# Transposes of both heads behind the value matmuls, in the first layer's attention

## The chip, the cores and the metric

The kernel runs on one core of a Trainium2 chip. The metric is the device time of one execution in microseconds. Lower is better. The engines are TensorE (PE in the rows, its weight loads PEld), VectorE (DVE), ScalarE (ACT), GpSimd (POOL) and SyncE (SP).

## What is computed

Two transformer layers on x of 2 x 1024 tokens by 128 features, all in f32. Each layer is attention and a feed-forward part, each with layer norms before and behind it. The first layer's attention, which the change is about:

```
q, k, v = proj(wq), proj(wk), proj(wv)          # 16 heads of 64
scores = einsum('bhqd,bhkd->bhqk', q, k) * 64 ** -0.5
scores = where(causal, scores, -inf)
probs = softmax(scores)
out = einsum('bhqk,bhkd->bhqd', probs, v)
return einsum('bse,he->bsh', out, wo)
```

Behind it come a mixture of 8 experts, an attention with 16 heads of 8 and rotary positions, and a ternary-weight feed-forward part.

## The kernel before

The first layer's 16 heads go in 8 turns of two heads (`HPC` is 2). A turn has 16 query tiles of 128 rows, 8 for each batch row b. A tile qt needs the keys of tiles 0 to qt, so its cost grows with qt + 1. The order of tiles in a turn is qt 0, 4, 1, 5, 2, 6, 3, 7 for b = 0 (the first half), then 7, 3, 6, 2, 5, 1, 4, 0 for b = 1: large tiles (qt 4 to 7) and small ones (0 to 3) alternate. A tile's two heads are a pair of items, the even head 2p and the odd head 2p + 1. Softmax sums are taken out at the end of each half.

An item passes through these operations (line numbers of the kernel before):

- scores on TensorE (L1100), a product with the high and one with the low part of the keys, into `pS`, which has two buffers, so that item i waits for the maximum of item i - 2
- maximum on VectorE (L828), which also writes the masked scores to `probs`, which has three buffers (`NPROB`): item i waits for the transposes of item i - 3
- exponential on ScalarE (L605), in place in `probs`, with its sum read out behind it
- transposes on TensorE (L1133), one for each key tile, at most four to a round. A round takes one of three banks `pT` (`TBANKS`) and waits for the copy of the round three before it. Items of large tiles take two rounds, of small ones one.
- copy of each round to `PT` in SBUF, by ScalarE (L585) or VectorE (L862), in turn by the number of the round
- value matmuls for both heads of a pair (L1063), then VectorE's copy of the result (L787)

The projections of the coming batch row or turn are rounds too ("P", L1025 for queries and keys, L1029 for values), twelve in a turn, copied by ScalarE (L553, L561). They stand at odd steps.

All engines run an in-order program that is written out step by step. `Attention.__init__` makes the table of rounds: `at_step[i]` lists the rounds of step i, and each engine's loop over i follows it. In an even step i TensorE issues the scores of items i and i + 1. In an odd step it issues the value matmuls of the pair i - 5, i - 4. In each step it then waits for the exponential of item i - 2 and issues the rounds of the table. ScalarE's step is its exponential of item i and then the copies of the step's rounds. VectorE's step is the output copy, the maximum of item i, and then its copies.

Of the kernel before, what the change touches and what calls it, by code (L numbers as in the profile page):

```python
# [24 lines left out]
T = B * S  # L25
# [3 lines left out]
TPB = BANK // P  # L29
# [3 lines left out]
HPC = P // DH0  # L33
# [49 lines left out]
class Attention:  # L83
# [3 lines left out]
    def __init__(self, heads, turns, copies, project):  # L87
        self.heads = heads
        tiles = list(range(ST)) if heads > 2 else [t + h * (ST // 2) for t in range(ST // 2) for h in range(2)]
        order = [(0, qt) for qt in tiles] + [(1, qt) for qt in reversed(tiles)]  # L90
        self.order = [(c, b, qt) for c in range(turns) for b, qt in order]
        self.items = [(c, b, qt, h) for c, b, qt in self.order for h in range(heads)]
        self.n = len(self.items)
        self.per = self.n // turns
        self.rounds = []
        self.at_step = [[] for _ in range(self.n + 8)]
        self.copied = {"act": 0, "dve": 0}
        self.round_of = {}
        self.done_by = []
        if project:  # L100
            for u in range(6):
                self.project(0, 0, 0, u)
            self.at_step[0] = []
        self.ahead = len(self.rounds)
        for step in range(self.n + 8):
            if 2 <= step < self.n + 2:
                c, b, qt, h = self.items[step - 2]
                for k0 in range(0, qt + 1, TPB):
                    self.add(step, "T", (step - 2, k0, min(TPB, qt + 1 - k0)), [copies[len(self.rounds) % len(copies)]])
                self.round_of[step - 2] = len(self.rounds) - 1  # L110
            if project:
                c, at = divmod(step, self.per)
                for c2, b2, start in ((c, 1, 1), (c + 1, 0, self.per // B + 1)):
                    u, odd = divmod(at - start, 2)
                    if 0 <= u < 6 and not odd and c2 < turns:
                        self.project(step, c2, b2, u)
            self.done_by.append(dict(self.copied))
# [1218 lines left out]
```

How the kernel before makes its waits and increments, by code:

```python
            def halves(c, b):  # L354
                lo, hi = slice(0, DH0), slice(DH0, P)
                if (c, b) == (0, 0):
                    sp.wait_ge(A[0]["cp_dve"], plan.projected(c, b, 0, 1, "dve"))
                else:
                    sp.wait_ge(split_step, 2 * HPC * (plan.split_number(c, b, 0, 1) + 1))
                sp.dma_start(Qs[hi, b, 0, :].bitcast(F32), Ql[lo, b, :].bitcast(F32)).then_inc(ld_half[b], 16)
                sp.dma_start(Qs[lo, b, 1, :].bitcast(F32), Ql[hi, b, :].bitcast(F32)).then_inc(ld_half[b], 16)
                if (c, b) == (0, 0):
                    sp.wait_ge(A[0]["cp_dve"], plan.projected(c, b, 1, 1, "dve"))
                else:
                    sp.wait_ge(split_step, 2 * HPC * (plan.split_number(c, b, 1, 1) + 1))
                for kx in (Kh, Kl):
                    sp.dma_start(kx[hi, b, 0, :].bitcast(F32), kx[lo, b, 0, :].bitcast(F32)).then_inc(ld_half[b], 16)
                    sp.dma_start(kx[lo, b, 1, :].bitcast(F32), kx[hi, b, 1, :].bitcast(F32)).then_inc(ld_half[b], 16)
# [1 line left out]
            def spread(half):  # L371
                sp.wait_ge(turned_copied, half + 1)
                sp.dma_start(factors[half, :, :].rearrange("h (t q) -> (h t) q", q=P), factorsT[:, :]).then_inc(factors_out, 16)
                if half == 0:
                    sp.wait_ge(q_p, 5 * (FC1 + 1))
                else:
                    sp.wait_ge(rescaled, half)
                sp.wait_ge(factors_out, 16 * (half + 1))
                for h in range(HPC):
```

## Time and profile before

| | us |
|---|---|
| median of 3 runs | 1271.85 (1269.1 to 1274.05) |
| profiled execution | 1276.66 |
| its span | 1274.7 |
| TensorE busy | 1114.3 (87%) |
| VectorE busy | 869.6 |
| ScalarE busy | 817.2 |
| GpSimd busy | 348.9 |

The first layer's attention lies at about 45 to 562 us of the span, the experts behind it, and the second layer's attention at about 830 to 1200 us. TensorE's records overlap, since matmuls are pipelined: the distance between starts is its pace, the mean duration is not.

### The profile page before, as it was taken

How to read it: one execution, taken by the hardware profiler on the slowest of the kernel's cores; microseconds unless marked ns; L12 is line 12 of the kernel's file. 1: busy time of each engine (PE TensorE's matmuls, PEld its weight loads, DVE VectorE, ACT ScalarE, POOL GpSimd, SP SyncE). 2: the span in 40 equal slices, each digit the busy share in tenths (PEclk: the TensorE clock that was granted, in tenths of full speed). 3: DMA queues.
4: the chain of work that ended last, by engine and by line, in shares of the span. 5: the costliest groups of instructions: out<-in, count | busy, mean ns of one | idle time of the engine just before them, and what ended most of it. 6: DMA issues, size and time to landing. Idle time of an engine off the chain costs nothing.

```text
span 1274.7 us, 28360 instructions
## 1 busy us (share of the span) xinstructions
PE 1114.3 (87%) x10202; PEld 850.3 (67%) x10202; DVE 869.6 (68%) x2512; ACT 817.2 (64%) x1915; POOL 348.9 (27%) x345
## 2 busy tenths in 40 slices
PE   2799999999999999998999951688888888888886
PEld 1587888787878787888676730456556556556674
DVE  3565656565656665645433476799899999999863
ACT  2566666666666666631434223789889989989832
POOL 1597464646464545313000051000000000000033
PEclk9899999999999999998899976799899999899998
DMA  3222232323232222211000004311302202100001
GB/s 107 70 60 62 69 73 59 83 57 84 57 76 66 69 72 68 67 35 42 5 17 25 5 1 118 56 24 17 39 12 29 38 4 37 27 14 2 2 1 33
DMA packets 29671, 56.74 MB, mean 45 GB/s; under 512 B 4538, under 2 KB 14674, under 8 KB 29410
## 3 DMA queue, kind: packets, MB, share of 16 engines
q1 hardware_dynamic: 28738, 53.43, 18.8%
q8 instruction: 80, 1.31, 0.4%
q10 hardware_dynamic: 800, 1.57, 0.4%
q14 instruction: 53, 0.43, 0.1%
HBM read 25.49 MB, written 4.33 MB: 23 GB/s over the span
## 4 chain that ended last, share of the span: by engine, by line
PE 55%; DVE 19%; issue 11%; ACT 6%; POOL 5%; DMA 3%; SPq 1%; ACTq 0%; POOLq 0%; DVEq 0%
PE pT L1133 12%; PE pO L1063 11%; PE pS L1100 10%; DVE Zb L818 9%; PE pS L1195 4%; PE pT L1025 4%; PE pT L1207 3%; DVE Sm L833 3%; ACT probs L605 3%; PE pS L1156 2%; PE pT L1029 2%; PE pS L1293 1%; PE pS L1273 1%; ACT PT L585 1%; DMA KS<-split 1%
## 5 line engine op out<-in xcount | busy, mean ns | idle before, releaser
L1133 PE MATMUL pT<-cst,probs 128*128 128x128 f32 x2304 | 368.8, 286 | 55.2 <-ACT probs L605 53.2
L1133 PEld LDWEIGHTS pT<-cst,probs 128*128 128x128 f32 x2304 | 255.5, 142 | 151.9 <-ACT probs L605 104.0
L605 ACT ACTIVATE probs<-probs,nmax 128x128 f32<-128x128 f32 (+7 forms) x256 | 198.8, 776 | 131.7 <-DVE nmax L828 130.7
L585 ACT COPY PT<-pT 128x512 f32<-128x512 f32 (+3 forms) x576 | 263.7, 481 | 16.1 <-PE pT L1133 14.7
L828 DVE CUSTOM_DVE_ANT_0 probs<-pS,causal_wide 128x128 f32<-128x128 f32 (+7 forms) x256 | 192.1, 750 | 92.8 <-PE pS L1100 85.2
L1063 PE MATMUL pO<-PT,V 128*64 128x128 f32 (+1 forms) x4608 | 230.6, 277 | 1.9 <-DVE attnT L787 1.1
L605 ACT ACTIVATE probs<-Sm,nmax 128x128 f32<-128x128 f32 (+7 forms) x256 | 199.2, 778 | 29.3 <-DVE nmax L833 22.3
L818 DVE TENSOR_SCALAR Zb<-pS 128x128 bf16<-128x128 f32 (+7 forms) x256 | 192.8, 753 | 24.4 <-PE pS L1106 24.1
L461 POOL TENSOR_TENSOR rstd<-rstd,power 128x4 f32<-128x4 f32 x32 | 32.8, 1025 | 628.0 <-DVE rstd L725 627.4
L1063 PEld LDWEIGHTS pO<-PT,V 128*64 128x64 f32 (+1 forms) x4608 | 179.9, 113 | 33.8 <-issue 19.6
L833 DVE CUSTOM_DVE_ANT_0 Sm<-pS,Zb 128x128 f32<-128x128 f32 (+7 forms) x256 | 193.3, 755 | 4.5
L862 DVE COPY PT<-pT 128x256 f32<-128x256 f32 (+3 forms) x192 | 99.9, 520 | 115.9 <-PE pT L1133 114.5
L1100 PE MATMUL pS<-Kh,Qs 128*128 128x512 f32 (+2 forms) x384 | 159.0, 423 | 7.2 <-DMA Kl<-Kl 7.2
L1100 PE MATMUL pS<-KS,QS 72*128 72x512 bf16 (+3 forms) x384 | 109.0, 338 | 36.0 <-DMA KS<-split 31.9
L1100 PE MATMUL pS<-Kl,Qs 128*128 128x512 f32 (+2 forms) x384 | 128.8, 344 | 0.0
L1100 PEld LDWEIGHTS pS<-Kh,Qs 128*128 128x128 f32 x384 | 73.3, 191 | 27.8 <-issue 21.7
L1100 PEld LDWEIGHTS pS<-Kl,Qs 128*128 128x128 f32 x384 | 73.5, 191 | 20.3 <-issue 14.6
L645 ACT ACTIVATE hT<-pS,b1e 128x512 f32<-128x512 f32 x64 | 43.9, 687 | 57.5 <-PE pS L1195 57.3
L504 POOL TENSOR_TENSOR Kl<-raw,Kh 64x512 fp32r<-64x512 f32 x60 | 76.5, 1276 | 4.8
L504 POOL TENSOR_TENSOR Ql<-raw,Qs 64x512 fp32r<-64x512 f32 x60 | 76.5, 1275 | 4.8
L524 POOL TENSOR_TENSOR attnT<-attnT,wq_t 128x1024 f32<-128x1024 f32 x16 | 37.9, 2370 | 117.6 <-DMA wq_t<-factors 117.0
L976 DVE SCALAR_TENSOR_TENSOR acc<-pT,wcol,acc 128x128 f32<-128x128 f32 x96 | 27.0, 344 | 61.7 <-PE pT L1207 61.7
(185 smaller groups left out, 1376.2 us busy)
## 6 DMA issues: line engine op xcount, KB each, us to landing
Qs<-Ql SPq DMA_DIRECT2D x32, 256.0 KB, 3.7
Kh<-Kh SPq DMA_DIRECT2D x32, 256.0 KB, 3.4
Kl<-Kl SPq DMA_DIRECT2D x32, 256.0 KB, 4.6
wq_t<-factors SPq DMA_DIRECT2D x32, 256.0 KB, 3.9
QS<-split SPq DMA_DIRECT2D x72, 64.0 KB
KS<-split SPq DMA_DIRECT2D x72, 64.0 KB
w0s<-in_w SPq DMA_DIRECT2D x8, 192.0 KB, 4.1
split<-parts SPq DMA_DIRECT2D x2, 768.0 KB, 3.5
```

The lines of the kernel that those rows point to most:

```text
L504: i = pool.tensor_tensor(low[h], source[rows[h], :], high[h].bitcast(F32), ALU.subtract)
L585: nc.scalar.copy(PT[:, g % 2, h, k0 * P:(k0 + nk) * P], pT[r % TBANKS][:, 0:nk * P])\
L605: nc.scalar.activation(probs[:, i % NPROB, 0:n], src[:, 0:n], ACT.Exp, bias=nmax[:, i % 4:i % 4 + 1], scale=-1.0, accum_out=total).then_in ...
L818: nc.vector.tensor_scalar(Zb[:, i % NMASK, 0:n], pS[i % 2][:, 0:n], 0.0, MASKED, ALU.is_equal, ALU.mult).then_inc(a["z"], 1)
L828: nc.vector.tensor_tensor_reduce(probs[:, i % NPROB, 0:n], pS[i % 2][:, shift(k, qt):shift(k, qt) + n], causal_wide[:, S - n:S], -1.0, 3e3 ...
L833: nc.vector.tensor_tensor_reduce(Sm[:, i % NMASK, 0:n], pS[i % 2][:, 0:n], Zb[:, i % NMASK, 0:n], -(DH1 ** -0.5), 3e38, ALU.add, ALU.min, ...
L862: nc.vector.tensor_copy(PT[:, gg % 2, hh, k0 * P:(k0 + nk) * P], pT[r % TBANKS][:, 0:nk * P])\
L1025: return nc.tensor.matmul(p, w0s[:, what, :], xnT[:, b * S + j * BANK:b * S + (j + 1) * BANK], start=True, stop=True)
L1063: m = nc.tensor.matmul(pO[rows, 0:P], v, PT[:, g % 2, h, kt * P:(kt + 1) * P], start=(kt == 0), stop=(kt == qt), skip_group_check=True)
L1100: m = nc.tensor.matmul(pS[i % 2][:, (off + c0) * P:(off + c1) * P], lhs, keys[:, b, h, c0 * P:c1 * P], start=(n == 0), stop=(n == len(rhs) ...
L1133: m = nc.tensor.transpose(pT[r % TBANKS][:, kt * P:(kt + 1) * P], probs[:, item % NPROB, (k0 + kt) * P:(k0 + kt + 1) * P], ident)
L1195: nc.tensor.matmul(bank[u % 4], w1s[:, buf, f * P:(f + 1) * P], xnT[:, j * BANK:(j + 1) * BANK], start=True, stop=True).then_inc(up_done, 1)
```

## The change

The table of rounds is made differently for a layer whose heads go in twos. The transposes of item i - 2 stood in step i, so the even head's in an even step behind the scores and the odd head's in the next step behind the value matmuls. Now both stand in the odd step. In the even step TensorE issues only scores. Line numbers below the change grow by 3. The second layer's attention has `heads` = 4 and takes the first branch, its old order.

```diff
         for step in range(self.n + 8):
-            if 2 <= step < self.n + 2:
-                c, b, qt, h = self.items[step - 2]
+            ready = [step - 2] if heads > HPC else [step - 3, step - 2] if step % HPC == 1 else []
+            for item in ready:
+                if not 0 <= item < self.n:
+                    continue
+                c, b, qt, h = self.items[item]
                 for k0 in range(0, qt + 1, TPB):
-                    self.add(step, "T", (step - 2, k0, min(TPB, qt + 1 - k0)), [copies[len(self.rounds) % len(copies)]])
-                self.round_of[step - 2] = len(self.rounds) - 1
+                    self.add(step, "T", (item, k0, min(TPB, qt + 1 - k0)), [copies[len(self.rounds) % len(copies)]])
+                self.round_of[item] = len(self.rounds) - 1
```

On TensorE, in the first turn, before, behind the scores of qt 3: the transposes of qt 6's even head (7, to banks pT2 and pT0), the values of qt 2, and the transposes of qt 6's odd head (pT1 and pT2). In brackets the semaphores that a row waits for, `a0_cp_act` and `a0_cp_dve` for copies, `a0_p` for exponentials.

```order
97 L1133 MATMUL pT2<-cst,probs_57 128x128 [waits a0_cp_dve,a0_p]
98 L1133 MATMUL pT2<-cst,probs_57 128x128 x3
99 L1133 MATMUL pT0<-cst,probs_57 128x128 [waits a0_cp_act]
100 L1133 MATMUL pT0<-cst,probs_57 128x128 x2
101 L1063 MATMUL pO<-PT0_55,V0_54 64x128 [waits a0_cp_dve,a0_cp_act,a0_n]
102 L1063 MATMUL pO<-PT0_55,V0_54 64x128 x5
103 L1133 MATMUL pT1<-cst,probs_57 128x128 [waits a0_cp_act,a0_p]
104 L1133 MATMUL pT1<-cst,probs_57 128x128 x3
105 L1133 MATMUL pT2<-cst,probs_57 128x128 [waits a0_cp_act]
106 L1133 MATMUL pT2<-cst,probs_57 128x128 x2
```

The same place with the change:

```order
97 L1066 MATMUL pO<-PT0_55,V0_54 64x128 [waits a0_cp_act,a0_cp_dve,a0_n,a0_p]
98 L1066 MATMUL pO<-PT0_55,V0_54 64x128 x5
99 L1136 MATMUL pT2<-cst,probs_57 128x128 [waits a0_cp_dve,a0_p]
100 L1136 MATMUL pT2<-cst,probs_57 128x128 x3
101 L1136 MATMUL pT0<-cst,probs_57 128x128 [waits a0_cp_act]
102 L1136 MATMUL pT0<-cst,probs_57 128x128 x2
103 L1136 MATMUL pT1<-cst,probs_57 128x128 [waits a0_cp_act]
104 L1136 MATMUL pT1<-cst,probs_57 128x128 x3
105 L1136 MATMUL pT2<-cst,probs_57 128x128 [waits a0_cp_act]
106 L1136 MATMUL pT2<-cst,probs_57 128x128 x2
```

The values moved ahead of all four rounds. The first and the fourth round both take pT2, and between them nothing but two rounds of transposes is left. The wait for exponentials stands at the values (for the even head) and at the first transposes (for the odd one).

On ScalarE, before, behind qt 6's two exponentials (128x896) to those of qt 7 (128x1024), with the exponentials of qt 3 (128x512) and the first round's copy of each head of qt 6:

```order
34 L605 ACTIVATE probs_57,den0<-probs_57,nmax 128x896 [waits a0_mx] x2
35 L585 COPY PT0_55<-pT0 128x384 [waits a0_o,a0_t]
36 L561 COPY V0_54<-pT1 128x512 [waits a0_t]
37 L605 ACTIVATE probs_57,den0<-probs_57,nmax 128x512 [waits a0_mx]
38 L585 COPY PT0_55<-pT2 128x512 [waits a0_o,a0_t]
39 L605 ACTIVATE probs_57,den0<-probs_57,nmax 128x512 [waits a0_mx]
40 L585 COPY PT0_55<-pT1 128x512 [waits a0_o,a0_t]
41 L605 ACTIVATE probs_57,den0<-probs_57,nmax 128x1024 [waits a0_mx]
```

With the change:

```order
32 L608 ACTIVATE probs_57,den0<-probs_57,nmax 128x896 [waits a0_mx] x2
33 L588 COPY PT0_55<-pT0 128x384 [waits a0_o,a0_t]
34 L564 COPY V0_54<-pT1 128x512 [waits a0_t]
35 L608 ACTIVATE probs_57,den0<-probs_57,nmax 128x512 [waits a0_mx] x2
36 L588 COPY PT0_55<-pT2 128x512 [waits a0_o,a0_t]
37 L588 COPY PT0_55<-pT1 128x512 [waits a0_o,a0_t]
38 L608 ACTIVATE probs_57,den0<-probs_57,nmax 128x1024 [waits a0_mx] x2
```

The copy from pT2 stood between the two exponentials of qt 3, and now stands behind both.

## Rows read from the trace of the kernel before

**Rows 1.** Busy time by engine, granted clock, DMA share, GB/s, one stretch
```profile
200.00:330.00 130.00, 129.75 (x1158) 105.40 (x1157) 79.07 (x217) 87.17 (x200) 69.73 (x68) 1.00 0.28 69
```
**Rows 2.** Waits of TensorE and its weight loads, 72 to 560 us
```profile
PE pS L1100 <- DMA Kl<-Kl: 0.5, 1, 0.5
PE pO L1063 <- DVE attnT L787: 0.5, 1, 0.5
PE pT L1133 <- ACT PT L585: 0.4, 1, 0.4
...
PEld pT L1133 <- ACT probs L605: 7.9, 46, 0.2
```
**Rows 3.** Timeline of TensorE and its loads: start, us, what, idle before
```profile
333.76 0.39 PE L1100 MATMUL pS<-Kh,Qs 128*128 128x512 f32 x1
333.99 0.40 PE L1100 MATMUL pS<-Kl,Qs 128*128 128x512 f32 x1
...
334.69 1.04 PE L1133 MATMUL pT<-cst,probs 128*128 128x128 f32 x8
335.66 1.09 PE L1063 MATMUL pO<-PT,V 128*64 128x128 f32 x16
337.61 1.02 PE L1025 MATMUL pT<-xnT,w0s 128*128 128x512 f32 x2
...
335.65 0.85 PEld L1063 LDWEIGHTS pO<-PT,V 128*64 128x64 f32 x16 [0.17 <-issue]
336.68 0.86 PEld L1133 LDWEIGHTS pT<-cst,probs 128*128 128x128 f32 x8 [0.17 <-ACT probs L605]
```
**Rows 4.** Line 796: duration ns min/median/max, first and last start us
```profile
L796 DVE RECIPROCAL rden<-den x16: 241/243/247, 76.0 to 558.6; 128x16 f32<-128x16 f32 x16
```
**Rows 5.** VectorE: groups by shape, 72 to 560 us, then timeline pieces
```profile
L828 DVE CUSTOM_DVE_ANT_0 probs<-pS,causal_wide 128x1024 f32<-128x1024 f32 x30 | 36.2, 1207 | 3.2 <-PE pT L1133 1.6 <-PE pS L1100 1.2
...
L828 DVE CUSTOM_DVE_ANT_0 probs<-pS,causal_wide 128x512 f32<-128x512 f32 x30 | 20.6, 686 | 14.0 <-PE pS L1100 13.8 <-issue 0.2
...
L828 DVE CUSTOM_DVE_ANT_0 probs<-pS,causal_wide 128x128 f32<-128x128 f32 x30 | 8.1, 270 | 0.5 <-PE pS L1100 0.5
...
326.14 0.08 DVE L828 DVE_READ_ACCUMULATOR2_ANT nmax<- 128x1 f32 x1
...
335.76 0.69 DVE L862 COPY PT<-pT 128x512 f32<-128x512 f32 x1 [0.57 <-PE pT L1133]
```
**Rows 6.** ScalarE: groups by shape, 72 to 560 us, then timeline pieces
```profile
L585 ACT COPY PT<-pT 128x512 f32<-128x512 f32 x109 | 62.4, 572 | 8.6 <-PE pT L1133 8.5
...
L605 ACT ACTIVATE probs<-probs,nmax 128x1024 f32<-128x1024 f32 x31 | 35.6, 1150 | 30.0 <-DVE nmax L828 30.0
...
L605 ACT ACTIVATE probs<-probs,nmax 128x512 f32<-128x512 f32 x30 | 21.7, 724 | 9.3 <-DVE nmax L828 9.3
...
L605 ACT ACTIVATE probs<-probs,nmax 128x128 f32<-128x128 f32 x30 | 12.0, 401 | 7.8 <-DVE nmax L828 7.8
...
L585 ACT COPY PT<-pT 128x128 f32<-128x128 f32 x15 | 3.7, 246 | 0.0
...
326.26 0.72 ACT L605 ACTIVATE probs<-probs,nmax 128x512 f32<-128x512 f32 x1 [0.44 <-DVE nmax L828]
326.89 0.19 ACT L605 ACTIVATION_READ_ACCUMULATOR probs<-probs,nmax 128x1 f32 x1
326.99 0.56 ACT L585 COPY PT<-pT 128x512 f32<-128x512 f32 x1
```
**Rows 7.** Timeline of ScalarE and TensorE's loads at a copy waited for
```profile
310.67 0.58 ACT L585 COPY PT<-pT 128x512 f32<-128x512 f32 x1
...
311.30 0.14 PEld L1133 LDWEIGHTS pT<-cst,probs 128*128 128x128 f32 x1 [0.17 <-ACT PT L585]
```
**Rows 8.** Second layer: busy time by engine and clock, two stretches
```profile
860.00:880.00 20.00, 17.76 (x260) 13.81 (x249) 19.83 (x36) 19.05 (x42) 0.00 (x0) 1.00 0.21 27
...
900.00:920.00 20.00, 17.03 (x129) 10.32 (x130) 16.30 (x72) 16.48 (x62) 0.00 (x0) 0.74 0.46 57
```

## Prediction

> **What bounds the kernel now.** I read the busy times by stretch first. In the first layer's attention (about 45 to 562 us) TensorE is busy for 129.75 of 130 us at a granted clock of 1.00, with VectorE at 79 and ScalarE at 87 us [rows 1]. That alone could be an illusion, since matmul ends are modelled, so next the waits: in 488 us TensorE's matmuls wait 0.5 us for a DMA, 0.5 us for VectorE and 0.4 us for ScalarE, and its weight loads 7.9 us for exponentials, never over 0.2 us at a time [rows 2]. So no chain through other engines is late: every result is there when TensorE's in-order program comes to it. Whatever the change takes from that slack is free until it is used up, and then costs in full, because the engines that would be waited for stand in series and TensorE has nothing else to issue.
>
> **TensorE's own pace.** In [rows 3] eight transposes (L1133) take 334.69 to 335.66, of which 8 x 0.107 us are streaming and about 0.11 the change to the value matmuls (L1063); those take 335.66 to 336.68 for 16 records (0.053 each) and 0.17 for the change back, as the weight loads' idle 0.17 shows. Value matmuls leave two records per instruction, so a tile with n key tiles costs 4n x 0.053 us. Scores (L1100) go at 0.23 per 512 columns (333.76 to 333.99), a 512-column projection (L1025) takes 0.86. By such intervals a turn (16 tiles, two heads each) sums to 62.0 us: scores 17.4, transposes 15.4, values 15.4, projections 8.6, about 0.28 of switching and 0.05 of first-score delay in each of 16 pairs. Measured are 15 halves between the reciprocals at 76.0 and 558.6 us, 64.3 us a turn [rows 4]. I keep the 2.3 us of difference as bubbles I cannot place.
>
> **What the change does.** Nothing is added or removed: same matmuls, exponentials, copies, DMAs; the second layer (`heads > HPC`) keeps its order. The switches between 128- and 64-column matmuls stay two a pair (scores to values, values to transposes), so the 0.28 us stays. SP's and GpSimd's queues keep their order; their transfers and splits follow the loop's pace, whatever that is. What moves is the even head's transposes, from before the value matmuls to behind them, and on ScalarE and VectorE the even head's copies, from before the odd head's exponential and maximum of the next pair to behind them. Call the pair whose transposes run P and the next pair N. Three waits change:
>
> (a) The odd maximum of N overwrites the `probs` buffer of P's even head (three buffers), so it waits for P's even transposes. These were issued right after the scores; now they stand behind the value matmuls.
>
> (b) `pT` has three banks, and a large tile (qt 4 to 7) needs two rounds a head, four a pair. The fourth round takes the bank of the first, so it waits for the first round's copy. Before, that copy was made between N's two exponentials, while the value matmuls ran. Now it stands behind N's odd exponential on ScalarE (or N's odd maximum on VectorE), which by (a) can't begin before P's even transposes are done. So within one block of transposes TensorE waits for: end of even transposes, odd maximum, odd exponential, copy. Nothing is left to cover it but one round of four transposes.
>
> (c) Even transposes now also wait for their own pair's odd exponential.
>
> **Cost of (b).** From the end of streaming of the even transposes: 0.21 us until the next engine can begin (335.55 to 335.76, [rows 3, 5]); the maximum m; 0.04 to the exponential (326.22 to 326.26) [rows 5, 6]; from its start to the copy's start x, which is the row's mean duration (326.26 to 326.99 for 0.724); the four-tile copy, 0.572; 0.05 until TensorE goes on (311.25 to 311.30) [rows 7]. Against it stand 4 x 0.107 of transposes. The stall is 0.44 + m + x. m is 0.270, 0.686, 1.207 for 1, 4 and 8 key tiles, x 0.401, 0.724, 1.150 [rows 5, 6]; between those I interpolate straight.
> A worked one, qt 6 in the first half, N being qt 3: 0.44 + 0.686 + 0.724 = 1.85 us.
> Banks and engines alternate by round number; counting rounds (6 ahead, then 60 a turn), the first round's copy is ScalarE's for the first half's large tiles and for qt 4 of the second. The others: qt 4 (N is qt 1) 0.44+0.41+0.51 = 1.36; qt 5 (N 2) 0.44+0.55+0.62 = 1.61; qt 7 (N is the other batch's qt 7) 0.44+1.21+1.15 = 2.80; second half's qt 4 (N 0) 0.44+0.27+0.40 = 1.11.
> For the second half's qt 7, 6, 5 VectorE copies the first round, and the projection round behind them waits for ScalarE's copy c of the second, which decides: 0.30 + m + x + c less the odd transposes already streamed. qt 7 (N 3): 0.30+0.69+0.72+0.57-0.86 = 1.43; qt 6 (N 2): 0.30+0.55+0.62+0.46-0.75 = 1.18; qt 5 (N 1): 0.30+0.41+0.51+0.36-0.64 = 0.94. The shorter copies c are on the line between 0.246 (one tile) and 0.572.
> Sum of a turn: 1.36+1.61+1.85+2.80+1.43+1.18+0.94+1.11 = 12.3 us.
> Small tiles need two rounds and never meet this wait.
>
> **Cost of (a) and (c).** After a small tile's transposes the next large pair's odd maximum and exponential follow, in place of which TensorE streams odd transposes, a projection, two scores and the small tile's values. For second-half qt 4 behind qt 1 without a projection: transposes 0.21, 0.21, maximum 0.82 give 1.24 plus about 0.05, while TensorE reaches the odd score (pS needs that maximum) at 0.43+0.28 = 0.71, so 0.6 late. For the others the same sum gives 0 to 0.2. Together 0.9 us a turn.
>
> **Sum.** 13.2 us x 8 turns = 105 us on the profiled execution's 1276.7, so 1382; the runs' median is 4.8 us under that execution, so **1377 us**. Bounds: if the 2.3 us a turn of unplaced bubbles lie where the stalls fall, 10.9 x 8 = 87 and 1359. If operations that here overlap by 0.09 (the copy at 326.99 starts before the read of the sum ends at 327.08) come one behind another, and ScalarE, which must first do the previous small copy, a projection copy (0.6) and N's even exponential, is itself late by some 0.4 in the five cases where it copies the first round, a turn costs 13.2 + 8 x 3 x 0.09 + 5 x 0.4 = 17.4, or 1411. The clock I leave at 1.00: the second layer's stretch at 17.76 of 20 us busy has it [rows 8], and the loop here would be busy for 64 of 78.
>
> **Rivals.**
> *Hidden after all.* The copies come earlier than I think, and only (a) and (c) cost: 0.9 x 8 = 7, so 1279. For it speaks that ScalarE and VectorE are idle a third of the time; against it that (b) is a chain in series, which idle engines don't shorten. 5%.
> *Faster.* One of the block changes disappears: transposes to values cost 0.11 us, 128 pairs x 0.11 = 14, so 1258. It needs scores to values to be free, and (b) to cost under 0.11 us a pair on average, where I have 0.8; above that it is slower. That the cause is the array's shape and not the instruction kind fits the 0.17 us in both directions. 3%. (The Trainium skill, "TensorEngine Tiling (Array Packing)", Key Properties, says that a change of tiling mode drains the engine; by that rule the new order keeps both drains and this rival is worth nothing.)
> *Clock.* The new stalls of 1 to 3 us cut TensorE's work into bursts and the granted clock falls. In a stretch of the second layer with heavy DMA traffic it was 0.74 [rows 8]; at that, 64.3 us of work in a turn become 87, +22.6 x 8 = 181 on top of 1377, so 1558. Against it: the second layer's other stretches keep 1.00 at 17 to 18 busy of 20 us [rows 8]. 5%. (The Trainium skill, "TensorE: Matmul & The Clock Gate", under the psum-queue depth-cycling failure, says that short idle spells between groups of matmuls, from cycling through banks, were seen to make the clock swing between its levels. By it the time would go towards this rival. The trace shows no such loop in the first layer.)
> *Slower by far less*: two thirds of the chain hidden by work I put in the wrong place, 1300 to 1340. 6%.
> The forecast's mechanism has the remaining 81%.
>
> **Numbers.** 1377 is the likeliest mechanism's time; 1345 to 1425 takes in both bounds with some room, and leaves the rivals, 19%, outside. A difference under 0.5% (6 us) can't be told from none. Faster 3% (that rival), same 3% (the better part of the hidden one), slower 94%.
>
> **What would show it.** Right: between 45 and 660 us TensorE waits for ScalarE's PT copies (L588) some 35 to 40 times by 1 to 3 us and for VectorE's or ScalarE's behind the rest; VectorE's maximum (L831) waits for transposes; reciprocals lie 38.7 us apart instead of 32.2; clock 1.00; everything behind the attention has its old lengths. Wrong: transposes without a wait between third and fourth round (then (b) is no chain), a granted clock under 0.9 there (the clock), or waits at the exponential larger than at the copies (then (c) is mis-sized).

## The result, and the profile after

The kernel with the change takes 1484.55 us (median of 4 runs, 1480.91 to 1487.43), against 1272.95 before: ratio 1.1663, interval 1.1621 to 1.1705. It is slower by 212 us. I had forecast slower by 105, 1377 in a range of 1345 to 1425. The direction is right, the size is not.

All of it lies in the first attention. VectorE's reciprocals come once a half, so the stretch between the first and the last of the 16 holds 7.5 turns. The first row is that line's in the kernel after, then come the busy times and the granted clock of that stretch:

```profile
L799 DVE RECIPROCAL rden<-den x16: 242/248/249, 84.5 to 772.9; 128x16 f32<-128x16 f32 x16
...
84.50:772.90 688.40, 533.11 (x4341) 413.52 (x4341) 288.53 (x811) 324.21 (x745) 248.84 (x242) 0.95 0.19 46
```

The stretch of before (76.0 to 558.6, [rows 4]) has this row:

```profile
76.00:558.60 482.60, 480.51 (x4326) 391.47 (x4322) 294.72 (x810) 323.13 (x745) 255.57 (x246) 1.00 0.27 66
```

It grew by 205.8 us: 153.2 of TensorE's idle time (155.3 against 2.1) and 52.6 of its busy time. ScalarE's and VectorE's busy times are the old ones, so nothing got longer there. The granted clock fell from 1.00 to 0.95, which I had left at 1.00. The waits of TensorE's matmuls in that stretch (us in total, times, longest), which answer to [rows 2]:

```profile
PE pT L1136 <- ACT PT L588: 64.5, 40, 2.7
PE pO L1066 <- ACT raw L556: 27.8, 21, 1.7
PE pO L1066 <- ACT V L564: 20.7, 14, 1.6
PE pT L1136 <- DVE PT L865: 20.0, 21, 1.1
PE pO L1066 <- ACT PT L588: 15.6, 18, 1.2
PE pS L1103 <- DVE nmax L831: 5.8, 10, 0.6
```

The reciprocals lie 45.9 us apart, where the forecast had 38.7. Three groups are to be seen. Transposes (pT) wait for copies 61 times, 84.5 us: the fourth round's wait, (b) of the prediction. Scores (pS) wait for the maximum, 5.8 us: the small wait I had for second-half tiles. And value matmuls (pO) wait 53 times for ScalarE's copies, 64.1 us, at small tiles (qt 0 to 3). That group is nowhere in the prediction.

**The fourth round, in the trace.** TensorE, ScalarE and VectorE of the kernel after, in the first half of a turn, from qt 6's transposes on (start, us, what, idle before):

```profile
349.91 1.42 PE L1136 MATMUL pT<-cst,probs 128*128 128x128 f32 x11
351.05 0.27 PE L1136 MATMUL pT<-cst,probs 128*128 128x128 f32 x1
353.11 0.55 PE L1136 MATMUL pT<-cst,probs 128*128 128x128 f32 x3 [1.78 <-ACT PT L588]
...
351.77 0.72 ACT L608 ACTIVATE probs<-probs,nmax 128x512 f32<-128x512 f32 x1 [2.21 <-DVE nmax L831]
352.40 0.18 ACT L608 ACTIVATION_READ_ACCUMULATOR probs<-probs,nmax 128x1 f32 x1
352.49 1.05 ACT L588 COPY PT<-pT 128x512 f32<-128x512 f32 x2
...
351.04 0.69 DVE L831 CUSTOM_DVE_ANT_0 probs<-pS,causal_wide 128x512 f32<-128x512 f32 x1 [2.94 <-PE pT L1136]
```

Eleven transposes run, three rounds; the second row is the last of them by itself. The odd maximum of qt 3 begins at 351.04, 2.94 us after VectorE last had work, the exponential at 351.77, the copy at 352.49, and TensorE goes on at 353.11. The last of the eleven starts at 351.05, and such records start 0.11 us apart, so its streaming ends at 351.16 and the hole is 1.95 us where 1.85 was predicted. The row shows 1.78, since the modelled end of the last matmul (351.05 + 0.27) lies 0.17 behind its streaming. I call these 0.17 us the hidden tail of a wait.

**The values' wait, in the trace.** The same three engines one pair earlier, qt 2's transposes and the values of qt 2 behind the scores of qt 3:

```profile
345.03 0.88 PE L1136 MATMUL pT<-cst,probs 128*128 128x128 f32 x6
345.74 1.06 PE L1032 MATMUL pT<-w0s,xnT 128*128 128x128 f32 x8
346.55 0.47 PE L1103 MATMUL pS<-Kh,Qs 128*128 128x512 f32 x1
...
349.10 0.88 PE L1066 MATMUL pO<-PT,V 128*64 128x128 f32 x12 [1.37 <-ACT V L564]
...
345.72 1.09 DVE L831 CUSTOM_DVE_ANT_0 probs<-pS,causal_wide 128x896 f32<-128x896 f32 x1 [1.77 <-PE pT L1136]
...
346.86 1.04 ACT L608 ACTIVATE probs<-probs,nmax 128x896 f32<-128x896 f32 x1 [1.74 <-DVE nmax L831]
...
347.90 0.46 ACT L588 COPY PT<-pT 128x384 f32<-128x384 f32 x1
348.26 0.58 ACT L564 COPY V<-pT 128x512 f32<-128x512 f32 x1
```

Qt 2's even transposes are the first three of the six from 345.03, and the odd maximum of qt 6, which waits for them, starts at 345.72. Its exponential starts at 346.86. Behind it ScalarE makes qt 2's copy and the projection's copy, until 348.84, and only then may the values start, at 349.10. The scores were issued from 346.55 on and had nothing left by 347.7. It is the same chain, transposes, odd maximum, odd exponential, copies, with another customer at its end.

**The clock, in the trace.** Three stretches of the kernel after around one of its eight longest stalls, and the work behind that stall:

```profile
360.00:364.00 4.00, 2.96 (x30) 2.17 (x28) 1.84 (x4) 2.14 (x5) 0.00 (x0) 1.00 0.00 0
364.00:368.00 4.00, 1.55 (x5) 1.25 (x6) 1.65 (x4) 2.20 (x4) 0.00 (x0) 0.77 0.00 0
368.00:372.00 4.00, 4.00 (x36) 2.76 (x36) 1.19 (x4) 1.41 (x3) 1.88 (x3) 0.81 0.02 4
...
366.45 1.12 PE L1136 MATMUL pT<-cst,probs 128*128 128x128 f32 x4 [2.74 <-ACT PT L588]
367.36 1.92 PE L1028 MATMUL pT<-xnT,w0s 128*128 128x512 f32 x2
368.29 1.40 PE L1103 MATMUL pS<-Kh,Qs 128*128 128x512 f32 x1
```

After 2.74 us without a matmul four transposes take 0.91 us to the next row instead of 0.43: the lower of the two levels, 1.2 GHz. The projection behind them is just as slow. Seven of the eight stalls of 2.74 us have such slow work behind them. Behind the one that ends at 456.83 the clock stayed at 1.00.

The clock also falls where no long stall is, in the second half of a turn, at qt 1 and the tiles behind it:

```profile
122.77 0.44 PE L1136 MATMUL pT<-cst,probs 128*128 128x128 f32 x2 [0.80 <-DVE PT L865]
128.25 0.38 PE L1103 MATMUL pS<-Kh,Qs 128*128 128x256 f32 x1 [0.58 <-DVE nmax L831]
129.67 0.66 PE L1066 MATMUL pO<-PT,V 128*64 128x128 f32 x8 [0.91 <-ACT PT L588]
...
128.00:132.00 4.00, 2.83 (x19) 2.23 (x19) 1.44 (x9) 1.80 (x6) 0.00 (x0) 0.83 0.01 4
132.00:136.00 4.00, 3.35 (x24) 2.99 (x25) 0.89 (x5) 1.72 (x6) 0.00 (x0) 0.50 0.00 0
136.00:140.00 4.00, 4.00 (x25) 2.62 (x22) 1.53 (x6) 1.58 (x5) 1.06 (x2) 0.82 0.00 0
```

From about 130.5 to 137.5 us the clock is at the lower level, behind three stalls of under 1 us each. This comes back at the same place in six of the first seven turns, and once elsewhere in the last turn (748 to 752 us, behind stalls of 0.51 and 1.22 us). The fifth turn has the same stalls there (0.58 and 0.91 us, at 405.15 and 406.56) and keeps 1.00. Read in half microseconds, each one's busy time times what its clock lacks of 1.00, the slow work sums to an estimated 31 us in the stretch: 11 behind seven of the long stalls and 20 at the other seven places.

### The profile page after: what moved, and what is told of

The parts are those of the page before. It is cut to its first block, busy times and chain, and to the rows that moved or that the text cites. A ratio compares the mean times of both kernels' runs of the same rounds, so it can differ in the third digit from the quotient of the medians.

```text
span 1485.5 us, 28357 instructions
## 1 busy us (share of the span) xinstructions
PE 1163.8 (78%) x10202; PEld 868.0 (58%) x10202; DVE 862.6 (58%) x2512; ACT 816.8 (55%) x1915; POOL 347.8 (23%) x345
## 4 chain that ended last, share of the span: by engine, by line
PE 47%; issue 20%; DVE 18%; ACT 10%; DMA 2%; POOL 1%; SPq 1%; DVEq 0%; ACTq 0%; POOLq 0%
PE pO L1066 12%; PE pT L1136 10%; DVE Zb L821 8%; PE pS L1103 7%; ACT PT L588 4%; ACT probs L608 4%; PE pT L1028 3%; PE pS L1198 3%; PE pT L1210 3%; DVE Sm L836 3%; PE pS L1159 2%; PE pS L1296 1%; DMA KS<-split 1%; PE pS L1276 1%; PE pO L1210 1%
## 5 line engine op out<-in xcount | busy, mean ns | idle before, releaser
L1066 PE MATMUL pO<-PT,V 128*64 128x128 f32 (+1 forms) x4608 | 237.4, 281 | 69.0 <-ACT raw L556 29.2
L588 ACT COPY PT<-pT 128x512 f32<-128x512 f32 (+3 forms) x576 | 259.2, 481 | 8.7 <-PE pT L1136 6.3
L1066 PEld LDWEIGHTS pO<-PT,V 128*64 128x64 f32 (+1 forms) x4608 | 187.2, 116 | 111.3 <-issue 58.8
L1103 PE MATMUL pS<-Kh,Qs 128*128 128x512 f32 (+2 forms) x384 | 168.3, 445 | 13.1 <-DMA Kl<-Kl 6.7
L1103 PE MATMUL pS<-Kl,Qs 128*128 128x512 f32 (+2 forms) x384 | 131.8, 350 | 0.0
L504 POOL CAST Qs<-raw 64x512 fp32r<-64x512 f32 x60 | 36.5, 608 | 269.6 <-ACT raw L556 267.2
L1028 PE MATMUL pT<-xnT,w0s 128*128 128x512 f32 x128 | 77.0, 691 | 1.1 <-ACT xnT L546 0.7
```

The source lines that it names most:

```text
L588: nc.scalar.copy(PT[:, g % 2, h, k0 * P:(k0 + nk) * P], pT[r % TBANKS][:, 0:nk * P])\
L1028: return nc.tensor.matmul(p, w0s[:, what, :], xnT[:, b * S + j * BANK:b * S + (j + 1) * BANK], start=True, stop=True)
L1066: m = nc.tensor.matmul(pO[rows, 0:P], v, PT[:, g % 2, h, kt * P:(kt + 1) * P], start=(kt == 0), stop=(kt == qt), skip_group_check=True)
L1103: m = nc.tensor.matmul(pS[i % 2][:, (off + c0) * P:(off + c1) * P], lhs, keys[:, b, h, c0 * P:c1 * P], start=(n == 0), stop=(n == len(rhs) ...
```

## The experiments

Eleven kernels ran. Each ratio is to the kernel before on the same chip. The edits are shown against the kernel with the change, and `...` stands for lines left out.

### Is the odd maximum's wait the root?

Four `probs` buffers in the first layer, the changed order. To make room, the weights of the first two experts share space with `Kl` and are loaded behind the attention.

```diff
-REGION = 160
+REGION = 164
...
+        self.nprob = 4 if heads == HPC else NPROB
...
-                        if i >= NPROB:
-                            dve.wait_ge(a["t"], plan.round_of[i - NPROB] + 1)
+                        if i >= plan.nprob:
+                            dve.wait_ge(a["t"], plan.round_of[i - plan.nprob] + 1)
```

> The order of the change, but with four probs buffers in the first layer, so that the odd maximum no longer waits for the even transposes of the pair before. (The weights of the first two experts are loaded behind the attention to make room.) Theory A, that this one wait is the root and the waits for copies at the fourth round and at the value matmuls only descend from it: the time comes back to that of before, 1262 to 1290 us, and the waits for copies in the first attention fall from 150 us to under 20. Theory B, that the copies' place behind both exponentials in ScalarE's order is enough by itself to make TensorE wait: 1340 us or more, with most of the waits for copies left.

Measured: 1307.09 us, ratio 1.0289 (1.0246 to 1.0332). Of 212 us 177 are gone with one more buffer and not one instruction moved on any engine's compute path. TensorE's waits in the stretch between the reciprocals:

```profile
PE pT L1137 <- ACT PT L589: 8.4, 14, 0.9
PE pO L1067 <- ACT raw L557: 7.0, 21, 0.6
PE pO L1067 <- DVE attnT L791: 3.2, 10, 0.5
PE pO L1067 <- ACT V L565: 2.8, 7, 0.4
```

The waits for copies are 18 us, as theory A had it, and B falls, though its queue order is unchanged here. But the time isn't back at 1272 and lies above A's range (1262 to 1290). A has a remainder of 35 us to explain.

The control has the same buffers and late load in the order of before.

> The order of before with four probs buffers and the late load of the experts' weights: the control for the kernel with four buffers in the new order, which took 1307. All theories: 1268 to 1276, since TensorE waits for nothing there. If this too is near 1305, the 35 us lie in the buffers or the late load, not in the order.

Measured: 1274.65 us, ratio 1.0012 (0.9993 to 1.0032). So the 35 us belong to the order.

### One part of the change alone

The rule that decides which even heads are moved, here for the large tiles; the small tiles' kernel has `< TPB`.

```diff
-            ready = [step - 2] if heads > HPC else [step - 3, step - 2] if step % HPC == 1 else []
+            late = lambda item: 0 <= item < self.n and self.items[item][2] >= TPB
+            if heads > HPC:
+                ready = [step - 2]
+            elif step % HPC == 1:
+                ready = [step - 3, step - 2] if late(step - 3) else [step - 2]
+            else:
+                ready = [] if late(step - 2) else [step - 2]
```

> Only the large tiles' (qt 4 to 7) even transposes are moved behind the value matmuls, the small tiles keep the order of before. If the fourth round's wait and the value matmuls' wait are separate costs (theory A): the bank waits stay (84 us), the value waits go, and with 10 to 25 us for the lower clock behind the long stalls the time is 1365 to 1385. If the two feed each other, either part alone costs clearly less than its share, so under 1350.

Measured: 1407.61 us, ratio 1.1057 (1.1015 to 1.1099), 22 us above the range. The waits of its stretch:

```profile
PE pT L1142 <- ACT PT L594: 67.4, 40, 2.7
PE pT L1142 <- DVE PT L871: 20.0, 21, 1.2
PE pO L1072 <- ACT raw L562: 8.0, 21, 0.7
```

The transposes' waits are those of the whole change (87.4 against 84.5), so the fourth round's wait belongs to the large tiles alone. What I had set too low was all that comes with it: busy time of 510.27 in the stretch against 480.51, and 14 us at the values. Its clock (0.98) falls only behind the eight longest stalls.

> Only the small tiles' (qt 0 to 3) even transposes are moved. Theory A: no fourth round is in them, so no bank wait; the value matmuls of the small tile wait for copies behind the large tile's odd exponential, about 65 us, and the odd scores 6 us: 1335 to 1355. My prediction on record had only 7 us for this part: 1275 to 1285.

Measured: 1326.14 us, ratio 1.0429 (1.0391 to 1.0468). It lies between the two numbers, nearer to theory A's. But the waits are not where I had put them:

```profile
PE pT L1142 <- ACT PT L594: 22.5, 46, 1.0
PE pS L1109 <- DVE nmax L837: 5.8, 10, 0.6
PE pO L1072 <- DVE attnT L796: 2.1, 7, 0.3
```

Not one is at the values for a copy. Here the large tile's even transposes still stand between the scores and the small tile's values. They wait for the late copies in the values' place, and cover part of the time. So the parts are not independent: alone they cost 135 and 54 us, 189 together, and the whole 212. Most of the 23 us between goes with the clock. By the same half microseconds the slow work is 12.5 us with the large tiles alone, none with the small tiles alone (the clock is 1.00 all through), and 31 with both.

### ScalarE's order

```diff
-                    if k == 0:
+                    if k == 0 and i % HPC == 0:
                         exponential(i)
                         rounds_out(i)
```

> The order of the change, but ScalarE makes the copies of an odd step before its exponential, not behind it; VectorE keeps its order. Theory A: the 65 us of waits for ScalarE's copies at the fourth round and most of the waits at the value matmuls go, those for VectorE's copies (20 us) stay, and the odd exponential, now behind the copies, makes the next transposes wait by some 0.5 to 1 us for large pairs: 1330 to 1400. Theory B, that ScalarE's order alone is the cause: 1275 to 1300.

Measured: 1346.99 us, ratio 1.0597 (1.0555 to 1.064). ScalarE's queue order is worth 138 us while the maximum is late, so it is a condition of the chain. (The clock of the stretch is 1.00 here, so the 138 us hold the 31 of slow work.) It isn't all of it: 75 us remain, and the rows name VectorE, whose copies still stand behind its odd maximum.

```profile
PE pT L1136 <- DVE PT L865: 20.0, 21, 1.2
PE pT L1028 <- DVE PT L865: 6.2, 7, 0.9
PE pS L1103 <- DVE nmax L831: 5.8, 10, 0.6
```

### The values' wait

The values of a pair one pair later in the first layer, so that their copies have more time.

```diff
+        self.queued = 6 if heads == HPC else QUEUED
...
-                    if plan.ends_group(i - QUEUED):
-                        values(k, plan.group(i - QUEUED), i)
+                    if plan.ends_group(i - plan.queued):
+                        values(k, plan.group(i - plan.queued), i)
```

> The order of the change, but in the first layer the value matmuls of a pair (and the copy of their result) come one pair later than now, so that the copies they wait for have one more pair's time. Theory A, that the values' wait for copies behind the odd exponential is the term missing from the prediction (64 us of waits by the trace, about 78 with the pipeline's tail): these waits vanish, the 84 us at the fourth round stay, and the time is 1390 to 1420. Theory C, that TensorE waits for the chain through maximum and exponential wherever the values stand: the wait only moves to the next transposes or scores, and the time is over 1450.

Measured: 1408.78 us, ratio 1.1069 (1.1042 to 1.1096), 75.8 us less than the change, as theory A had it. Its rows have no wait for a copy at the values, and at the transposes the old ones:

```profile
PE pT L1137 <- ACT PT L589: 66.7, 40, 2.7
PE pT L1137 <- DVE PT L866: 19.8, 21, 1.1
PE pS L1104 <- DVE nmax L832: 6.1, 10, 0.9
```

Theory C, that the wait only moves on, falls. The 75.8 us aren't the values' wait alone, though: the stretch's clock rose from 0.95 to 0.98. All eight long stalls still have slow work behind them, the other places have none, and the slow work is 13 us where it was 31. On the other side TensorE has 9 us more idle time elsewhere (100.0 us in all, where 155.3 less the 64.1 would leave 91.2).

The projection's copy by itself: `done_by` is recorded ahead of the projections of a step, so that the values wait for the transposes' copies alone.

```diff
+            self.done_by.append(dict(self.copied))
             if project:
...
-            self.done_by.append(dict(self.copied))
```

> The order of the change, but the value matmuls wait only for the copies up to the transposes of their step, not for the projection's copy behind them. Of the 53 waits at the values 35 ended with a projection's copy, which takes about 0.5 us behind the transposes' copy on ScalarE: 17 us less, 1460 to 1475. If those waits are really for the exponential ahead of them all, at most this; if nothing changes (over 1480), they are for VectorE's copy, which ends at about the same time.

Measured: 1448.93 us, ratio 1.1379 (1.1346 to 1.1411), 36 us less than the change and twice what I expected. The waits did what was expected: 46.7 us at the values for copies, 17.4 less than 64.1. The rest is in the busy time, 517.35 against 533.11, at a clock of 0.98 against 0.95. With the shorter waits the clock stayed up more. (The profile is of the slowest of its four runs, 1457.81 us.)

The control for the later values, in the order of before:

> The order of before with the value matmuls one pair later, the control for the two kernels that have it: TensorE waits for nothing in the first attention either way, so 1268 to 1278.

Measured: 1314.22 us, ratio 1.0344 (1.0314 to 1.0373). The expectation missed it by 36 us. Waits in 80 to 560 us:

```profile
DVE PT L863 <- PE pO L1064: 137.9, 75, 2.8
...
ACT PT L586 <- PE pO L1064: 63.9, 54, 1.9
```

`PT` has two buffers, so a copy waits for the values of the pair two before. With the values one pair later, in the old order the even head's transposes come ahead of just those values: their copies can't be made, and the banks stay full. The transposes wait 23.6 us for copies in the stretch (0.4 before). In the changed order the transposes stand behind the values, and the setback doesn't arise. Distance helps there and hurts here.

### The clock

Eight dummy transposes in front of each large pair's third round. They add work to TensorE, and their result is overwritten.

```diff
-                        for r in plan.at_step[i]:
+                        for at, r in enumerate(plan.at_step[i]):
...
+                                if k == 0 and at == 2 and plan.items[item][2] >= TPB:
+                                    for _ in range(8):
+                                        nc.tensor.transpose(pT[r % TBANKS][:, 0:P], cst[:, C_UPPER:C_UPPER + P], ident)
```

> The order of the change plus eight dummy transposes (0.86 us of TensorE's time, result overwritten) ahead of each large pair's third round, that is inside the stall before the fourth round (0.9 to 2.8 us). If the granted clock of 0.95 costs nothing: 1480 to 1490, since the dummies fill waiting time. Theory A, that idle spells of 2 to 3 us lower the clock and the slow work behind them costs some 20 us: the clock rises towards 1.00 and the time falls to 1462 to 1478. If the dummies are not hidden: 1484 + up to 64 x 0.86 = 1539.

Measured: 1466.25 us, ratio 1.1536 (1.1502 to 1.157), 18.3 us less than the change, with more work. The stretch, and the first of its waits:

```profile
82.70:748.60 665.90, 559.64 (x4829) 447.56 (x4829) 289.56 (x811) 323.74 (x745) 248.97 (x242) 1.00 0.19 48
...
PE pT L1139 <- ACT PT L588: 32.4, 39, 1.9
```

The clock is back at 1.00 with the 27.6 and 20.7 us of waits at the values still there, and one slow piece is left (126.7 to 130.7 us). The dummies take the place of idle time at every fourth round: its waits fall from 84.5 to 34.0 us, the longest from 2.7 to 1.9 us and those for VectorE's copies from 20.0 to 1.6. So it is idle time before the fourth round without which the clock hardly falls. This run doesn't tell the long stalls from the short ones, and the trace of the change has slow work behind both.

### What is left with four buffers

> The order of the change with four probs buffers and with the value matmuls one pair later. With four buffers alone it took 1307, with 13 us of waits at the value matmuls, 8 us for ScalarE's copies at the transposes and 13 us more busy time than before. Theory A: the values' waits go with the greater distance, the 8 us stay: 1285 to 1295, not under the kernel before. If a burst of both heads' transposes costs nothing in itself and the rest of the 35 us was all at the values: 1268 to 1278.

Measured: 1291.17 us, ratio 1.0144 (1.0117 to 1.0171). Later values take 16 of the 35 us.

> As the kernel with four buffers and later values, and ScalarE makes an odd step's copies before its exponential. The remaining waits at the fourth round were for copies that stood behind an exponential (8 us of waits, some 15 with the pipeline's tail): 1272 to 1284. If it is over 1290, the rest of the loss lies in the burst itself: a round's copy (0.57 us) against the three rounds of transposes that cover it.

Measured: 1292.77 us, ratio 1.0176 (1.015 to 1.0203). ScalarE's order is worth nothing any more: the 4.8 us that transposes waited for its copies are gone, and 4.6 us for its now later exponentials have come. A queue order that cost 138 us behind a late maximum costs none behind an early one. Its stretch is 504.0 us long, against 482.6 before. The wait for a copy or an exponential that is left in it:

```profile
PE pT L1138 <- ACT probs L610: 4.6, 7, 0.7
```

That some 20 us remain, mostly in gaps too short to be listed as waits, I read as the burst's own price: a first round's copy needs 0.21 + 0.57 + 0.05 = 0.83 us, and the rounds that cover it are back to back. The waits of the weight loads, which stand ahead of the matmuls, point the same way: 12.0 us for copies of transposes, 37 times and never over 0.4, where the kernel before has 1.8, and 17.0 us for exponentials, where it has 7.9. That is 19 us more, but no run takes the burst apart by itself, so the reading is argued, not shown. No version here beats the kernel before.

## Why the prediction was wrong

The forecast was 105 us slower, the result is 212.

**The chain (b) and its price were right.** The prediction summed it to 12.3 us a turn, 98 for eight. The stretch begins behind qt 4, 5 and 6 of the first turn, so 93 for its 61 waits. Measured are 84.5 us of waits and 61 hidden tails of 0.17, 95 us, and by an estimate from three of them (those that end at 98.31, 111.40 and 122.77 us) another 2 to 3 before the projection rounds behind, about 98. One by one: 1.95 measured for 1.85 at qt 6, and 2.90 for 2.80 at qt 7:

```profile
363.44 0.27 PE L1136 MATMUL pT<-cst,probs 128*128 128x128 f32 x1
366.45 1.12 PE L1136 MATMUL pT<-cst,probs 128*128 128x128 f32 x4 [2.74 <-ACT PT L588]
```

The 0.10 too little in both is one step: from the end of the even transposes to the odd maximum it takes 0.31 us (350.73 to 351.04), and the prediction had taken 0.21 from a copy. Its root was right too, (a): one more buffer removed 177 of 212 us.

**The step that failed is "Cost of (a) and (c)".** It said that after a small tile "TensorE streams odd transposes, a projection, two scores and the small tile's values", and priced only the odd score's wait for the maximum (0.6 us forecast; the row at 128.25 has 0.58, 0.75 with its tail). It passed over the values themselves. They wait for the copies of the pair and of the projection round behind it, and these copies stand behind the odd exponential by the same delay as in (b). With 0.9 us a turn it had 7 us for this whole part. The values' waits alone are 64.1 us and 53 tails of 0.17 (the scores ahead of them have the same tail, 347.33 + 0.40 against 347.33 + 0.23), 73 us. The forecast's own sentence on what moves, "the even head's copies, from before the odd head's exponential", names the delay, and I priced it for one of its two customers.

**"The clock I leave at 1.00"** failed as well. The reason given was that the second layer holds 1.00 at 17.76 busy of 20 us, but [rows 8] has a stretch at 17.03 of 20 beside it with 0.74, so the busy share alone didn't tell the two apart. The slow work is an estimated 31 us, and the filler got 18.3 back. Part of the difference is that waits behind slow work are shorter: the fourth round of the second half's qt 4 waits 0.65 us at 132.79, where the clock is low, and 1.06 at 409.41, where it isn't. The rival on the clock had named the cause, but its 181 us took 0.74 for the whole stage. (The Trainium skill, "TensorE: Matmul & The Clock Gate", in the part on psum-queue depth-cycling, tells of a clock that swings when TensorE idles between groups. This trace agrees in kind, with 0.77 and 0.81 behind a stall of 2.74 us, and 0.50 behind stalls of 0.80, 0.58 and 0.91 us.) What exactly makes the clock fall stays open: the same stalls had slow work behind them in most turns and not in the fifth.

**Sum.** In the stretch 98 (fourth round), 73 (values), 31 (clock) and 7.5 (scores, with their tails) make some 209, where it grew by 205.8 us. The first part agrees with the forecast within some 5%; the second and the third are in no term of it. An experiment that takes one part away moves the others too, so its gain isn't that part: the 75.8 us of the later values hold some 18 of the clock.

**The rivals.** Hidden after all, or slower by far less: no, 212 us. Faster: no; with both waits out of the way the order is still 1.4% slower. That rival needed scores to values to be free. They aren't: the last score before the values of qt 7 starts at 355.12, such scores go at 0.23 us, and the values start at 355.44, 0.09 later, against the 0.10 or so between transposes and values before.

## What to carry to other kernels

When work is moved behind something on an in-order engine, list everyone who waits for what it produces, and price the chain for each. The first customer found is seldom the only one, and here the second cost three quarters of the first. A loop at 99.6% busy can hang on one spare buffer: before a reorder look which buffer's release it delays, and follow that release through every queue back to the bound engine. A stall of TensorE can cost more than its length, since the work behind it can run slow. Look at the granted clock in short stretches and not only behind the longest stalls: here an estimated two thirds of the slow work stood behind stalls of 1.2 us and less.

## What the runs showed that I had not expected

- More work made the kernel faster: 8 dummy transposes at each of 61 places in the stretch, 0.86 us a time, took 18.3 us off and brought the granted clock from 0.95 to 1.00.
- The clock fell at fourteen places of the stretch, seven of them behind stalls of 1.2 us and less, and stayed up behind one of eight equal stalls of 2.74 us.
- The idle time a row gives for TensorE is 0.17 us less than the hole in its streaming (1.78 against 1.95 at 353.11). With 125 waits that is some 21 us that the profile counts as busy.
- Setting values one pair later gained 75.8 us in the changed order and lost 44 in the old one (1314.22 against 1270.54), through the two buffers of `PT`.
